# First mixture of experts: a fixed expert for 32 of 39 blocks, weights fetched in pairs during the attention before, and rows asked for two groups in front

## The reference, cut to what matters

```python
def _swiglu(x, gw, uw, dw):
    return jax.nn.silu(x @ gw) * (x @ uw) @ dw
x = hidden_states.reshape(-1, h)                      # 1024 x 128
shared_out = _swiglu(x, shared_gate_w, shared_up_w, shared_down_w)
logits = x @ gate_w                                   # 32 experts
topk_ids = jnp.argmax(logits, axis=-1)
topk_val = jnp.max(logits, axis=-1)
xs = x * jax.nn.sigmoid(topk_val)[:, None]
order = jnp.argsort(topk_ids)
sorted_x = xs[order]
g = _grouped_mm(sorted_x, routed_gate_w, tokens_per_expert)   # 128 -> 256
u = _grouped_mm(sorted_x, routed_up_w, tokens_per_expert)     # 128 -> 256
d = _grouped_mm(jax.nn.silu(g) * u, routed_down_w, tokens_per_expert)
return (shared_out + d[inv]).reshape(b, s, h)
```

## Time and profile before

| | |
|---|---|
| median of three runs | 1402.85 us (1401.79 to 1403.32) |
| the profiled execution | 1400.26 us, its span 1398.5 us |
| mean granted TensorE clock | 0.901 of full speed |
| TensorE busy in the span | 1162.0 us (83%) |
| first mixture, first to last expert matmul | from 250.86 us to about 321.5 us of the span |

### The profile page before, as it was taken

The page is one execution under the profiler, slowest core; times in us unless marked ns, Lnnn a source line. Parts: engine busy times, 40 slices in busy tenths (PEclk is TensorE's granted clock), DMA queues, the critical chain, the costliest instruction groups (busy, mean ns, idle before and its releaser), DMA issues.

```text
span 1398.5 us, 26578 instructions
## 1 busy us (share of the span) xinstructions
PE 1162.0 (83%) x9412; PEld 718.5 (51%) x9412; DVE 887.8 (63%) x2331; ACT 711.8 (51%) x1456; POOL 273.5 (20%) x558
## 2 busy tenths in 40 slices
PE   4988997784796499768999999999944978989994
PEld 2334344783343398555667666666634832333332
DVE  5767975335667443887676666777740166777866
ACT  3665882222633123415666665676712525646674
POOL 3522112352010265100000000000014404212220
PEclk9788999997797599989999999999966967999998
DMA  7321243893502486300000000011034834211200
GB/s 193 95 67 47 66 128 129 255 288 124 127 1 98 158 281 217 134 1 1 1 1 1 1 0 2 9 46 46 24 107 120 273 113 108 64 51 47 54 9 15
DMA packets 91620, 122.46 MB, mean 88 GB/s; under 512 B 11329, under 2 KB 69390, under 8 KB 90510
## 3 DMA queue, kind: packets, MB, share of 16 engines
q1 hardware_dynamic: 87266, 112.11, 26.2%
q0 software_dynamic: 4224, 8.66, 1.9%
HBM read 89.73 MB, written 30.02 MB: 86 GB/s over the span
## 4 chain that ended last, share of the span: by engine, by line
PE 62%; DVE 13%; DMA 8%; issue 6%; ACT 5%; POOL 3%; SPq 3%; DVEq 0%; ACTq 0%; POOLq 0%
PE ps L2641 7%; PE ps L2648 7%; PE ps L1168 7%; PE ps L2656 6%; PE ps L918 4%; PE ps L1797 3%; PE ps L927 3%; PE ps L1810 2%; PE ps L2730 2%; PE ps L1080 2%; PE ps L2737 2%; DMA probs<-in_L_ffn_w 2%; DMA wring<-in_L_ffn_w 2%; PE ps L1203 2%; PE ps L1799 2%
## 5 line engine op out<-in xcount | busy, mean ns | idle before, releaser
L1168 PE MATMUL ps<-probs,vaug 128*32 128x256 f32 (+1 forms) x1792 | 145.5, 400 | 12.1 <-ACT probs L1132 7.9
L2848 DVE CUSTOM_DVE_ANT_0 wring<-ps,probs 128x768 f32<-128x768 f32 x128 | 122.5, 957 | 46.5 <-PE ps L2641 45.9
L2807 ACT COPY qs<-ps 128x768 f32<-128x768 f32 x128 | 102.3, 800 | 90.4 <-PE ps L2648 90.4
L1123 ACT ACTIVATE probs<-ps 128x512 f32<-128x512 f32 x192 | 104.2, 595 | 64.5 <-PE ps L968 64.3
L273 POOL TENSOR_TENSOR rstd<-veps,mhalf 128x4 f32<-128x4 f32 (+2 forms) x28 | 26.5, 948 | 537.2 <-DVE veps L241 502.6
L1000 DVE TENSOR_REDUCE mx<-ps 128x2 f32<-128x1024 f32 (+1 forms) x96 | 115.4, 1219 | 18.8 <-PE ps L918 18.1
L1127 ACT ACTIVATE probs<-ps 128x512 f32<-128x512 f32 x192 | 104.7, 594 | 38.6 <-PE ps L1080 37.4
L2788 ACT ACTIVATE wring<-wring,r 128x768 f32<-128x768 f32 x128 | 120.8, 944 | 3.9 <-DVE r L2851 3.9
L2648 PE MATMUL ps<-ident,wring 128*128 128x128 f32 x768 | 110.2, 280 | 3.3 <-DVE wring L2892 3.2
L2648 PEld LDWEIGHTS ps<-ident,wring 128*128 128x128 f32 x768 | 83.4, 140 | 42.0 <-issue 35.4
L2052 POOL DMA_INDIRECT scr_y<-probs x85 | 82.1, 966 | 100.5 <-DVE probs L2006 95.2
(11 more groups left out here) (366 smaller groups left out, 2350.6 us busy)
## 6 DMA issues: line engine op xcount, KB each, us to landing
wring<-in_L_ffn_w SPq DMA_DIRECT2D x19, 768.0 KB, 6.3
wring<-in_L_ffn_w SPq DMA_DIRECT2D x32, 384.0 KB, 4.2
wring<-in_L_ffn_w SPq DMA_DIRECT2D x19, 514.0 KB, 5.2
probs<-scr_x SPq DMA_DIRECT2D x14, 256.0 KB, 4.2
qs<-scr_q SPq DMA_DIRECT2D x18, 192.0 KB
qs<-scr_qx SPq DMA_DIRECT2D x16, 192.0 KB
probs<-in_L_ffn_w SPq DMA_DIRECT2D x8, 384.0 KB, 4.1
probs<-in_L_ffn_w SPq DMA_DIRECT2D x4, 768.0 KB, 6.8
```

The source lines that it names most:

```text
L1123: act.activation(probs[:, s % 2, 2 * c + r, kt0 * S:(kt0 + 2) * S], bank(self.banks(3, k)[r]), ACT.Exp).then_inc(p_exp.sem, 1)
L1168: ins = pe.matmul(ps[32 * j:32 * j + 32, self.av_bank(s), q0:S], vaug[:, s % 2, kt, j, :], probs[:, s % 2, j, at:at + S - q0], start=(kt = ...
L2807: act.copy(self.pT[:, g % 2, j, :, k * P:(k + 1) * P], self.buffer("turn", i, 0, KV).rearrange("p (t n) -> p t n", n=P)).then_inc(self.out ...
L2848: dve.tensor_tensor_reduce(self.sc[:, s, :], src, self.maskb[:, u // (2 * PR), :], 1.0, -3.0e38, ALU.add, ALU.max, self.top[:, s:s + 1]).t ...
```

## The change

Four things are done.

1. **A fixed expert.** In the first mixture block e of the first 32 has expert e, whatever the routing says; it takes the first 128 tokens of that expert. The seven blocks behind them (32 to 38) serve the experts with more than 128 tokens, and only their experts are read from `expert_of`. `place_vector` gets one small operation more before `expert_of` (blocks needed, less one, not under zero), and its one operation that made the slots becomes four.
2. **Weights in pairs.** The weights of two blocks make one transfer of 768 KB into one of ten `lanes`, which lie in `wring`'s second slot, `qs` and `ks`. Twenty pairs in all. Pairs 0 to 2 are issued in the last step of the attention before, ahead of the wait for the late inputs and of the fill; pairs 3 to 9 as soon as its score matmuls are done (`ahead_sync`); pairs 10 to 19 in the loop, pair 10 + b // 2 when the odd block b is through its down projection. The last four pairs are issued as single blocks, with the expert from a register.
3. **Rows.** SP asks for group 0 and 1 when the rows are sorted, for group 2 when block 1 is done, and for group g + 3 when block 4g + 3, the last of group g, is done. A request stands ahead of the pair that is asked for at the same block.
4. **Counters.** Some counters of later sub-layers are shared with lanes, with their totals moved. Nothing else about them differs.

The other two mixtures keep their five slots. The core of the diff:

```diff
                 if self.n == 1 and g == G - 1:
+                    for p in range(3):
+                        mixtures[2].lane_sync(sp, p)
                     sp.wait_ge(loaded, LOADED)
...
+    W0 = 3 * 256
+    FIRST = MOES[0]["experts"]
+    LANES = 10
+    pairs0 = FIRST // 2 + -(-(blocks[0] - FIRST) // 2)
+    qsf0, ksf0 = qs[:, :].bitcast(F32), ks[:, :].bitcast(F32)
+    lanes = [wring[:, 1, :], *(qsf0[:, 4480 + i * 2 * W0:4480 + (i + 1) * 2 * W0] for i in range(2)),
+             *(ksf0[:, i * 2 * W0:(i + 1) * 2 * W0] for i in range(5)), *(qsf0[:, i * 2 * W0:(i + 1) * 2 * W0] for i in range(2))]
...
+        def lane_sync(self, sp, p):
+
+            sp.dma_start(lanes[p % LANES].rearrange("p (o n) -> p o n", o=2),
+                         self.packed[1 + 2 * p:3 + 2 * p].rearrange("o p n -> p o n")).then_inc(pair_in[p % LANES].sem, 16)
+
+        def ahead_sync(self, sp):
+
+            sp.wait_ge(b_mm.sem, b_mm.at(1, G * units[1]))
+            for p in range(3, LANES):
+                self.lane_sync(sp, p)
+
+        def first_sync(self, sp):
+
+            m = self.m
+            sp.wait_ge(sorted_out.sem, sorted_out.at(m, self.choices * NT))
+            for g in range(self.held):
+                self.x_sync(sp, g)
+            sp.wait_ge(placed.sem, placed.at(m, 1))
+            for b in range(1, self.nb, 2):
+                p, g = LANES + b // 2, b // self.gb + 1 + self.held
+                sp.wait_ge(down_mm.sem, down_mm.at(m, self.sh // 2 + b + 1))
+                if b % self.gb == self.gb - 1 and g < self.ng:
+                    self.x_sync(sp, g)
+                if b == 1:
+                    self.x_sync(sp, self.held)
+                if p >= pairs0:
+                    continue
+                if p < FIRST // 2:
+                    self.lane_sync(sp, p)
+                    continue
+                for i in range(min(2, self.nb - 2 * p)):
+                    extra = 2 * p + i - FIRST
+                    expert = sp.value_load(expert_of[extra:extra + 1, 0:1], min_val=0, max_val=self.e - 1 + self.shared)
+                    sp.dma_start(lanes[p % LANES][:, i * W0:(i + 1) * W0],
+                                 self.packed[bass.ds(expert, 1), :, :].rearrange("o p n -> p (o n)")
+                                 ).then_inc(pair_in[p % LANES].sem, 16)
...
             do(dve.tensor_scalar(need, need, ROUND, ROUND, ALU.add, ALU.subtract))
+            if self.shared:
+                do(dve.tensor_scalar(need, need, 1.0, 0.0, ALU.subtract, ALU.max))
...
+                do(dve.scalar_tensor_tensor(out=extra, in0=off, scalar=-1.0, in1=down[:, 0:e], op0=ALU.add, op1=ALU.add))
+                do(dve.scalar_tensor_tensor(out=block, in0=rank, scalar=float(P), in1=extra.unsqueeze(1).to_broadcast([P, NT, e]),
+                                            op0=ALU.is_gt, op1=ALU.mult))
+                do(dve.tensor_tensor(block, block, down[:, 33:33 + e].unsqueeze(1).to_broadcast([P, NT, e]), ALU.add))
+                do(dve.scalar_tensor_tensor(out=L, in0=block, scalar=float(P), in1=rank, op0=ALU.mult, op1=ALU.add))
+            else:
+                do(dve.scalar_tensor_tensor(out=L, in0=off.unsqueeze(1).to_broadcast([P, NT, e]), scalar=float(P),
+                                            in1=rank, op0=ALU.mult, op1=ALU.add))
...
                 subs[s].maxima_sync(sp)
+                if s == 1:
+                    mixtures[2].ahead_sync(sp)
```

More of the change, by code:

```diff
@@ L1561, in program @@
     m3 = range(3)
+    W0 = 3 * 256
[5 more added lines that the diff above has]
+             *(ksf0[:, i * 2 * W0:(i + 1) * 2 * W0] for i in range(5)), *(qsf0[:, i * 2 * W0:(i + 1) * 2 * W0] for i in range(2))]
+    pair_loads = [sum(1 if p < FIRST // 2 else min(2, blocks[0] - 2 * p) for p in range(i, pairs0, LANES)) for i in range(LANES)]
     sh = [4 * m["shared"] for m in MOES]
@@ L1619, in __init__, with weights @@
             self.ids = ids.rearrange("p (i w n) -> p i w n", w=2, n=self.nb)
-        def weights(self, r):
-            w, n = wslot[r % WS], self.width
+        def weights(self, b):
+            n = self.width
+            if self.shared and b < 0:
+                w = wslot[0]
+            elif self.shared:
+                w = lanes[b // 2 % LANES][:, b % 2 * W0:(b % 2 + 1) * W0]
+            else:
+                w = wslot[b % WS]
             if self.relu:
@@ L1626, in weights, with landed @@
             return w[:, 0:n], w[:, n:2 * n], w[:, 2 * n:3 * n], None
+        def landed(self, b):
+            if not self.shared:
+                return w_in[b % WS].sem, w_in[b % WS].at(self.m, b // WS + 1)
+            p = b // 2
+            lane = p % LANES
+            count = p // LANES + (1 if p < FIRST // 2 else min(2, self.nb - 2 * p))
+            return pair_in[lane].sem, pair_in[lane].at(0, count + (lane == LANES - 1))
+        def lane_sync(self, sp, p):
[29 more added lines that the diff above has]
+                                 ).then_inc(pair_in[p % LANES].sem, 16)
         def group(self, g):
@@ L1663, in sync @@
                 constant_rows(sp)
[L1664 to L1671, removed]
+            if self.shared:
+                self.first_sync(sp)
+            else:
+                sp.wait_ge(placed.sem, placed.at(m, 1))
+            for b in range(0 if self.shared else self.nb):
+                if b >= WS:
+                    sp.wait_ge(down_mm.sem, down_mm.at(m, b - WS + 1))
+                expert = sp.value_load(expert_of[b:b + 1, 0:1], min_val=0, max_val=self.e - 1)
+                sp.dma_start(wslot[b % WS][:, 0:n], self.packed[bass.ds(expert, 1), :, :].rearrange("o p n -> p (o n)")
+                             ).then_inc(w_in[b % WS].sem, 16)
                 if self.sorted:
@@ L1761, in shared_down_tensor @@
             m = self.m
-            last = self.weights(0)[2]
+            last = self.weights(-1)[2]
             pe.wait_ge(hid_sb.sem, hid_sb.at(m, self.sh))
@@ L1787, in up_tensor @@
             m, k = self.m, self.sh + b
-            r = b + self.shared
-            gate, up, _, _ = self.weights(r)
-            pe.wait_ge(w_in[r % WS].sem, w_in[r % WS].at(m, r // WS + 1))
+            gate, up, _, _ = self.weights(b)
+            pe.wait_ge(*self.landed(b))
             pe.wait_ge(x_T.sem, x_T.at(m, b // self.gb + 1))
@@ L1802, in down_tensor @@
         def down_tensor(self, pe, b):
-            m, last = self.m, self.weights(b + self.shared)[2]
+            m, last = self.m, self.weights(b)[2]
             pe.wait_ge(hid_sb.sem, hid_sb.at(m, self.sh + b + 1))
@@ L1848, in scalar @@
                         act.wait_ge(down_mm.sem, down_mm.at(m, self.sh // 2 + b - 1))
-                    bias = self.weights(b + self.shared)[3]
+                    bias = self.weights(b)[3]
                     for c in range(self.c):
```

35 lines of the change are left out of this document (19 added, 16 removed).

## The result

| | before | after |
|---|---|---|
| median of ten runs | 1397.97 us (1394.11 to 1403.32) | 1384.52 us (1383.28 to 1396.63) |
| profiled execution | 1400.26 us, span 1398.5 | 1389.44 us, span 1387.6 |
| mean granted TensorE clock, profiled execution | 0.901 | 0.906 |

The ratio of the runs is 0.9911, with an interval of 0.9886 to 0.9937: 12.4 us faster, between 8.8 and 15.9 (the two medians differ by 13.45). The forecast was 10.2 us faster, and that holds. The absolute time does not: 1384.5 us lies under the range of 1390.9 to 1397.0. The ten runs of before hold the three that the prediction started from; their median is 1397.97 and not 1402.85 us.

What follows compares the result with a forecast made beforehand. The prediction took the first mixture's loop to be fed weights too slowly, with the DMA engines idle ahead of it. Terms -11.5 + 1.3 and nothing for rows gave -10.2: 1402.85 to 1392.7 us, range 1390.9 to 1397.0.

Steps and rivals of the forecast that it cites:

- Part 1: Placing ahead of the loop: the fixed expert's four added operations delay POOL's scatters and everything behind, +1.3 us.
- Part 2: First mixture's loop: weights fetched early in pairs are never late, which removes TensorE's waits, -11.5 us.
- a step (1.34): Loop of the first mixture: one block with all data there takes 1.34 us, read from ScalarE's SiLU starts.
- a turn (0.44): Loop of the first mixture: a step with a turn in it takes 0.44 us more, 1.78.
- The rate: Transfers from 213.5 us on: 10.4 MB at 321 to 365 GB/s, done between 242 and 246 us.
- Part 3: Requests for rows, sharing the queue with the weight pairs: no wait expected, or one of under 2 us.
- The margins that I called narrow: Row requests in the loop: group 2 has 0.8 us spare; group 7 needs 6.6 us of 7.1 allowed.
- A: Rival: weight traffic delays rows before the loop or at group 2 or 7; 1393.7 to 1397.7 us, chance 0.24.
- C: Rival: late rows hold every group, slower once landings exceed 9.3 us; 1415 us with landings of 12, chance 0.03.
- B: Rival: something other than weights holds the loop, only the 1.3 us are added; 1401 to 1404 us, chance 0.05.
- D: Rival: gain above forecast, by cheap placing (0.5 us) and a start losing less; 1391.5 us, within the forecast's 0.65 chance.

Runs made afterwards that it cites:

- third trace: The changed kernel unaltered, run and traced a third time beside the kernel before: 1389.96 us, ratio 0.9933 to the kernel before.
- singles: The changed kernel with each pair of weights issued as two transfers of 384 KB in the same lane: 1388.95 us, ratio 0.9925 to the kernel before.
- spares: The changed kernel with twelve spare matmuls on TensorE while it waits for group 0's rows: 1390.34 us, ratio 0.9932 to the kernel before.

## Why the prediction missed the time and met the change

- **The base.** This is the step that failed: "the median of the runs lies 2.6 us above that execution, so 1402.85 - 10.2". I took three runs with a spread of 1.5 us for the time of the kernel, and built the range around them with 0.6 us for the runs' own spread. Over 28 runs on one chip the same kernel went from 1394.55 to 1407.85. The medians of before were 1397.97, 1398.86 and 1400.17 us; 1398.9 - 10.2 = 1388.7 would have been the forecast, and the medians of after, 1384.5, 1387.4 and 1390.0, lie around it. The base explains 4.9 of the 8.2 us by which 1384.5 lies under 1392.7. The other 3.3 are the measured time against 1397.97 - 10.2 = 1387.8: the traces show 0.6 of it in the mixture (10.8 for 10.2), and for the rest no cause is shown. A range for a time must hold the spread of the base, here some 5 us (1402.85 for three runs, 1397.97 for the ten that hold them), whatever the mechanism is.
- **Part 1**, +1.33 us: the scatter came 1.34 us later in the trace, and 1.36 later again when the operations were doubled. Missed was that a fixed expert spares SyncE the register read ahead of each request; the fixed expert alone gave 3.5 us in a loop that hangs on turnaround. In the changed kernel no wait for weights is left for it to shorten.
- **Part 2**, -11.5 us: 63.23 to 51.63, 11.6. "The next thing that is late in the loop is TensorE itself" held, it is busy throughout. The price of a step (1.34) and of a turn (0.44) held to the hundredth. What I did not see is which property does it. The head start, to which most of the working went, is worth about 3 us; the rest came without it, with ten blocks of depth, quicker requests and earlier rows together, and with three lanes the head start does not save the loop.
- **The rate** was mis-sized. The prefetch ran at 397 to 417 GB/s, not 321 to 365, and was through soon after 240 us, which is 238 to 239 in the times of before, not 242 to 246; the full stretch of the loop went at 350. What bound the loop before was the slots' turnaround, so its 321 GB/s for full engines was no ceiling. The Trainium skill ("DMA: Bandwidth & Descriptors", section Bandwidth) gives 425 GB/s for large transfers of a core that streams alone, and about 358 where both of a pair run. The rows of the prefetch lie near the first and above the second; the loop's 350 lies just under the second.
- **Part 3**, no wait: true in the traces of after. The margins that I called narrow were wider: asking two blocks later made waits for rows of 1.3 us in all.
- **Missed**: the copy of results waits for a scatter of four blocks before. I had read the ring's eight places and not its four counters. It costs 0 to 1 us.
- **Rivals.** A and C did not come; C's limit of 9.3 us was not neared, rows landed in 2.5 to 6.4 us over the whole of the three executions. B did not come. D came in part, and not by its cheap placing: the turn of group 0 came 0.94 us later against the copy of the logits (+24.61 for +23.67) and not 1.33, the start took 7.41 us for 7.63, and the loop gave 11.6 for 11.5. In the third trace the start took 6.84 us.

## What to carry to other kernels

Before a range is set around an absolute time, look at how far runs of the same program differ, and put that into it; three runs that agree are not yet a base. When a loop waits for loads, count how long a slot takes from its release to its next use (end of the block, request, landing) and how many blocks of work lie in that time: depth cures that, a head start only the first blocks. And read a ring's counters, not only its places: four counters for eight places make it wait like a ring of four.

## What the hardware showed that was not expected

- The head start, weights fetched from HBM in rows of 3 KB with the fill of `scr_x` among them, ran at 397, 403 and 417 GB/s in three stretches of 9 us beside work on all engines, and with singles at 419 and 405 in two.
- A register read ahead of a DMA on SyncE adds 0.72 us to a request (1.20 against 0.48 us from the down projection's entry to the load's). Whether the 3.5 us which the loop gained come from this alone was not tried.
- With 2.5 us of spares, a gap of 1.2 us on TensorE, the turn, and a gap of 0.7 us, the granted clock stood at 0.99 until 253.6 us and then at 0.50 for 2.8 us. With both gaps filled it did not fall. Which of the two gaps matters was not tried.
- Two executions of one program differ by 3.9 and 5.8 us in two stretches of 100 and 175 us, with granted clocks of 0.87 and 0.91 in the longer one, where only TensorE's busy time differs (154.79 and 148.00 us). Which of the two causes the other was not tried.
